# First head group of a decoder layer: turned rows in the output projection's bank, and another order of the first loads

## The reference, cut to what matters

```python
def _L0_attn_ref(x, wq, wk, wv, wo, q_scale, k_scale):     # x is the layer-normed input
    q = jnp.einsum('bse,ehd->bshd', x, wq)
    k = jnp.einsum('bse,ehd->bshd', x, wk)
    v = jnp.einsum('bse,ehd->bshd', x, wv)
    qn = rms_norm(q, q_scale)
    kn = rms_norm(k, k_scale)
    scores = jnp.einsum('bqhd,bkhd->bhqk', qn, kn)
    attn = jax.nn.softmax(scores, axis=-1)
    out = jnp.einsum('bhqk,bkhd->bqhd', attn, v)
    return jnp.einsum('bqhd,hde->bqe', out, wo)
x = x + _L0_attn_ref(_layernorm(x, axis=-1), ...)
```

## Time and profile before

| | |
|---|---|
| median of 3 runs | 2606.91 us (2603.4 to 2607.54) |
| profiled execution | 2602.67 us, its span 2600.9 us |
| TensorE busy | 2476.5 us, 95% |
| VectorE, ScalarE, GpSimd busy | 1544.2, 1343.1, 867.8 us |
| granted TensorE clock, mean | 0.98 of 2.4 GHz |

### The profile page before, as it was taken

How to read it: one execution, slowest core, us unless ns; L and a number is a source line. 1 busy time by engine, 2 the same in 40 slices (tenths; PEclk the granted TensorE clock), 3 DMA queues, 4 the chain that set the end, 5 groups by cost and what they waited for, 6 DMA issues and landing times.

```text
span 2600.9 us, 47418 instructions
## 1 busy us (share of the span) xinstructions
PE 2476.5 (95%) x16390; PEld 1334.4 (51%) x16390; DVE 1544.2 (59%) x3589; ACT 1343.1 (52%) x4098; POOL 867.8 (33%) x801
## 2 busy tenths in 40 slices
PE   6999999999999999999879999999999999999998
PEld 3555455555554555445454464464464464465466
DVE  7787756666666666667356545555554645645634
ACT  4555555555555555555446544454454554554433
POOL 2343333333333333333123324323323323422413
PEclk9999999999999999999869999999999999999999
DMA  5687777876787678787411001001001001000000
GB/s 155 151 183 169 154 154 158 175 166 148 156 173 156 154 157 185 167 193 162 125 35 34 32 3 35 16 2 37 17 2 37 12 6 37 4 14 24 7 17 8
DMA packets 455394, 235.29 MB, mean 90 GB/s; under 512 B 389096, under 2 KB 391784, under 8 KB 455144
## 3 DMA queue, kind: packets, MB, share of 16 engines
q1 hardware_dynamic: 455144, 232.08, 38.3%
HBM read 78.66 MB, written 32.77 MB: 43 GB/s over the span
## 4 chain that ended last, share of the span: by engine, by line
PE 84%; DVE 7%; ACT 4%; issue 3%; POOL 1%; DMA 1%; SPq 1%; DVEq 0%; POOLq 0%; ACTq 0%
PE ps L1474 22%; PE ps L1475 22%; PE ps L1476 22%; PE ps L1647 3%; PE ps L1648 2%; PE ps L1649 2%; ACT mem L948 2%; PE ps L1748 2%; PE ps L1657 1%; PE ps L1661 1%; PE ps L1659 1%; PE ps L1585 1%; PE ps L1736 1%; PE ps L1710 1%; PE ps L1730 1%
## 5 line engine op out<-in xcount | busy, mean ns | idle before, releaser
L1474 PE MATMUL ps<-mem 128*128 128x512 f16 (+6 forms) x3924 | 1203.5, 326 | 50.4 <-issue 23.3
L1475 PE MATMUL ps<-mem 128*128 128x512 f16 (+6 forms) x3924 | 1216.6, 325 | 0.0
L1476 PE MATMUL ps<-mem 128*128 128x512 f16 (+6 forms) x3924 | 1199.9, 325 | 0.0
L1474 PEld LDWEIGHTS ps<-mem 128*128 128x128 f16 (+3 forms) x3924 | 407.0, 104 | 370.8 <-issue 66.1
L1476 PEld LDWEIGHTS ps<-mem 128*128 128x128 f16 (+3 forms) x3924 | 408.4, 104 | 311.5 <-issue 9.2
L1475 PEld LDWEIGHTS ps<-mem 128*128 128x128 f16 (+3 forms) x3924 | 409.8, 104 | 300.4 <-issue 9.6
L736 POOL TENSOR_TENSOR mem<-mem 128x500 f32<-128x500 f32 (+1 forms) x231 | 268.6, 1163 | 358.3 <-ACT mem L1016 174.4
L686 POOL TENSOR_TENSOR mem<-mem 128x8 f32<-128x8 f32 x100 | 163.7, 1637 | 517.3 <-DVE mem L1090 517.3
L830 ACT ACTIVATE mem<-ps,mem 100x100 f32<-100x100 f32 x512 | 169.2, 345 | 223.2 <-DVE mem L1120 222.1
L1428 DVE TENSOR_TENSOR mem<-mem 128x500 f16<-128x500 f32 (+1 forms) x231 | 144.4, 648 | 179.7 <-ACT mem L998 175.3
L698 POOL TENSOR_TENSOR mem<-mem 100x400 f16<-100x400 f32 x128 | 158.8, 1241 | 173.1 <-ACT mem L840 173.1
(11 more groups left out here) (123 smaller groups left out, 3134.4 us busy)
## 6 DMA issues: line engine op xcount, KB each, us to landing
x<-mem SPq DMA_DIRECT2D x100, 256.0 KB, 2.9
mem<-x SPq DMA_DIRECT2D x75, 256.0 KB, 3.4
mem<-in_x SPq DMA_DIRECT2D x50, 256.0 KB, 3.6
mem<-x SPq DMA_DIRECT2D x12, 1000.0 KB
mem<-mem SPq DMA_DIRECT2D x32, 200.0 KB
out<-mem SPq DMA_DIRECT2D x6, 1000.0 KB
mem<-in_wq SPq DMA_DIRECT2D x16, 256.0 KB, 4.0
mem<-in_wk SPq DMA_DIRECT2D x16, 256.0 KB, 4.4
```

Of the source, the lines that this page charges most:

```text
L1474: pe.matmul(out_ap, ah, bh, start=(i == 0), stop=False)
L1475: pe.matmul(out_ap, ah, bl, start=False, stop=False)
L1476: mm = pe.matmul(out_ap, al, bh, start=False, stop=(i == len(pairs) - 1))
```

## The change

Rows are turned in the output projection's bank `ps_w` in place of the round of banks 0 to 3, so `UNITS` has only q and k. The turn waits for the adds of all output projections before it (`wo_before`), and an output projection waits for the `rows_lo` of all tiles turned before it (`rows_before`). `rows_lo` moves ahead of `scale_q` in VectorE's step. The eight quarters of q and k load in step -7, behind tile 1. Pieces q and k are split quarter by quarter, each with a semaphore of its own, on ScalarE and VectorE.

```diff
@@ -270,7 +270,7 @@
         ps = ctx.enter_context(nc.psum_tensor("ps", [P, 8, 512], F32))
         ps_v, ps_s, ps_w, ps_o = (ps[:, b, :] for b in range(4, 8))
 
-        names = ("ident0 ident half scales qks wld0 wld1 whi wlo xin0 xin1 xin2 bst mv var rstd xn lnT xhi "
+        names = ("ident0 ident half scales qks wq0 wq1 wq2 wq3 wk0 wk1 wk2 wk3 whq wld0 wld1 whi wlo xin0 xin1 xin2 bst mv var rstd xn lnT xhi "
                  "xlo qp kp sqq sqk ss ms rr qf khi klo qhi qlo qkT0 qkT1 vp ve vb0 vb1 s mx exp den rden "
                  "norm phi plo pz pT0 pT1 vlo o ohi olo w xr0 xr1 xr2 add st0 st1 st2")
         s = {n: sem("s_" + n) for n in names.split()}
@@ -301,12 +301,11 @@
 
         UNITS = []
         for n in range(FIRST_STEP, STEPS):
-            UNITS += [("rows", u) for u in turned_tile(n)]
             UNITS += [(m, u) for u in projected_at(n) for m in ("q", "k")]
 
         def bank(kind, u):
 
-            return ps[:, UNITS.index((kind, u)) % 4, :]
+            return ps_w if kind == "rows" else ps[:, UNITS.index((kind, u)) % 4, :]
 
         def bank_before(kind, u):
 
@@ -314,6 +313,15 @@
             return UNITS[i - 4] if i >= 4 else None
 
 
+        def wo_before(u):
+
+            return sum(len(summed_at(n)) for n in range(projected_step(u) - 1))
+
+        def rows_before(w):
+
+            at = [n for n in range(STEPS + 2) if w in summed_at(n)][0]
+            return sum(projected_step(u) - 1 <= at for u in range(TILES))
+
         def split_step(piece):
 
             hg, m = divmod(piece, 4)
@@ -321,7 +329,7 @@
 
         def load_step(piece):
 
-            return ((FIRST_STEP, FIRST_STEP, -4, -2)[piece] if piece < 4
+            return ((FIRST_STEP + 1, FIRST_STEP + 1, -4, -2)[piece] if piece < 4
                     else max(split_step(piece - 2) + 1, split_step(piece) - 4))
 
         def pieces_split(n):
@@ -537,7 +545,7 @@
                 if k >= 2:
                     sp.wait_ge(s["wlo"], k - 1)
                 sp.dma_start(stages[:, k % 2, e, :], piece_src(k)[:, e, :]
-                             ).then_inc(s[f"wld{k % 2}"], 16)
+                             ).then_inc(s[f"wld{k % 2}" if k >= 2 else f"w{'qk'[k]}{e}"], 16)
 
             def load_x(u):
                 if u >= 3:
@@ -764,8 +772,15 @@
 
         @block.scalar
         def _(act):
+            def split_first_hi(k):
+
+                for e in range(KC):
+                    act.wait_ge(s[f"w{'qk'[k]}{e}"], 16)
+                    act.activation(piece(k, True)[:, e, :], stages[:, k, e, :], ACT.Copy,
+                                   scale=W_SCALE).then_inc(s["whq"], 1)
+
             def split_hi(k):
-                act.wait_ge(s[f"wld{k % 2}"], 16 * KC * (k // 2 + 1))
+                act.wait_ge(s[f"wld{k % 2}"], 16 * KC * (k // 2))
                 if k >= 8:
                     act.wait_ge(s["w"], TILES * (k // 4 - 1))
                 act.activation(piece(k, True), stages[:, k % 2, :, :], ACT.Copy,
@@ -907,7 +922,7 @@
                 if 0 <= n + 1 < STEPS:
                     probs_hi(n + 1)
                 for k in pieces_split(n):
-                    split_hi(k)
+                    split_first_hi(k) if k < 2 else split_hi(k)
                 for k in b_pieces_split(n):
                     split_b_hi(k)
                 for u in projected_at(n):
@@ -1035,8 +1050,18 @@
 
         @block.vector
         def _(dve):
+            def split_first_lo(k):
+
+                for e in range(KC):
+                    dve.wait_ge(s["whq"], KC * k + e + 1)
+                    op = dve.scalar_tensor_tensor(out=piece(k, False)[:, e, :],
+                                                  in0=stages[:, k, e, :], scalar=W_SCALE,
+                                                  in1=piece(k, True)[:, e, :], op0=ALU.mult,
+                                                  op1=ALU.subtract)
+                op.then_inc(s["wlo"], 1)
+
             def split_lo(k):
-                dve.wait_ge(s["whi"], k + 1)
+                dve.wait_ge(s["whi"], k - 1)
                 dve.scalar_tensor_tensor(out=piece(k, False), in0=stages[:, k % 2, :, :],
                                          scalar=W_SCALE, in1=piece(k, True),
                                          op0=ALU.mult, op1=ALU.subtract).then_inc(s["wlo"], 1)
@@ -1225,16 +1250,16 @@
                     inverse_sum(n + 1)
                 for u in valued_at(n):
                     take_v_lo(u)
+                for u in turned_tile(n):
+                    rows_lo(u)
                 for u in projected_at(n - 1):
                     scale_q(u)
                 for u in projected_at(n - 1):
                     split_qk(u)
                 for u in normed_tile(n):
                     ln_rows(u)
-                for u in turned_tile(n):
-                    rows_lo(u)
                 for k in pieces_split(n):
-                    split_lo(k)
+                    split_first_lo(k) if k < 2 else split_lo(k)
                 for k in b_pieces_split(n):
                     split_b_lo(k)
                 for u in projected_at(n):
@@ -1480,11 +1505,14 @@
 
                 before = bank_before(kind, u)
                 if before:
-                    pe.wait_ge(s[{"rows": "xlo", "q": "qf", "k": "klo"}[before[0]]], before[1] + 1)
+                    pe.wait_ge(s[{"q": "qf", "k": "klo"}[before[0]]], before[1] + 1)
 
             def turn_rows(u):
                 pe.wait_ge(s["xn"], u + 1)
-                bank_free("rows", u)
+                if u:
+                    pe.wait_ge(s["xlo"], u)
+                if wo_before(u):
+                    pe.wait_ge(s["add"], wo_before(u))
                 for e in range(KC):
                     mm = pe.transpose(bank("rows", u)[:, e * P:(e + 1) * P], xin[:, u % 3, e * P:(e + 1) * P],
                                       ident[:, :])
@@ -1553,6 +1581,7 @@
                 pe.wait_ge(s["olo"], hg * NB + (t * P + P - 1) // S + 1)
                 if w:
                     pe.wait_ge(s["add"], w)
+                pe.wait_ge(s["xlo"], rows_before(w))
                 at = w * P % ORING
                 three(ps_w[:, :], [(oT_hi[:, h, at:at + P], oT_lo[:, h, at:at + P], out_hi[:, h, :],
                                     out_lo[:, h, :]) for h in range(HG)]).then_inc(s["w"], 1)
```

## The result

| | median | lowest to highest | runs |
|---|---|---|---|
| before | 2604.82 us | 2601.02 to 2611.19 | 17 |
| after | 2596.35 us | 2591.79 to 2601.28 | 17 |

The ratio is 0.9964, 95% interval 0.9957 to 0.9971: faster by 0.36%, where the prediction had 15.8 of 2606.9, 0.61%. By the medians 8.5 us went. The direction and the range held (2585 to 2599); the size is about half of the sum. All medians and ratios here are of executions at the usual granted clock, a mean of 0.975 to 0.982; one execution of experiment e7 and two of before, at 0.65 to 0.83, are left out. The profiled execution of after has a span of 2595.2 us, against 2600.9.

The account below looks back on a forecast made before the run. TensorE, busy 95% of the span, was taken as the bound, so only its stops count. 5.4 + 0.6 + 10.1 - 0.3 = 15.8 us off the 2606.91 median gave 2591.1 us, range 2585 to 2599.

Parts of the forecast that it names:

- Part 1: Opening: tile 1 loaded second and weights split by quarters start the first projection at 11.5 instead of 16.92: 5.4 us.
- Part 2: Behind the first projection: `rows_lo` moved ahead of `scale_q` saves 0.6 us; the wait ending at 55.32 ends 6.0 earlier.
- leave the clock at zero: Slow matmuls behind the longer stop (about 2 us) against the slow stretch behind 55.32 (1.7 us): counted as zero.
- Part 3: Five later waits for `scale_q` in the first group, 1.5 to 2.5 us each, go entirely: 10.1 us.
- neither a transpose nor an add takes their place: Rival, chance 0.10: transposes or adds are late instead of `scale_q`, leaving only the opening's 6.0 us: 2600.9.
- Part 4: Added waits between turning tiles and output projections in the shared bank: cost 0.3 us in all, upper end 5.1.
- list of what would make it wrong: Signs: turns waiting for adds, or output projections for `rows_lo`, over 1 us in total; new transpose stops; clock under 0.9.
- more than counted: Rival, chance 0.07: the 3.70 us stop for a late transfer and its slow matmuls go, 4 to 5 us more: 2586.5.
- theory A: From the experiments, not the forecast: the losses behind the first group are the scatter of executions.

Follow-up runs that it names:

- e7: Changed kernel, with rows turned in the next k projection's bank in steps without q and k projections, plus 34 one-element VectorE memsets ahead: 2587.30 us, ratio 0.9929.
- e4: Changed kernel, but in steps without q and k projections rows are turned in the next k projection's bank: 2592.57 us, ratio 0.9951.
- e12: Changed kernel with 34 memsets and rows turned in k's bank in steps without q and k projections, except tile 18: 2587.97 us, ratio 0.9927.
- e5: Kernel before with only the new banks and `rows_lo` order, plus six one-element VectorE memsets ahead of its loop: 2600.74 us, ratio 0.9979.
- e2: Kernel before with only the new banks and `rows_lo` order, loads and weight splits as before: 2595.97 us, ratio 0.9963.
- e3: Kernel before with only the new load order and split by quarters, old banks and `rows_lo` place: 2604.25 us, ratio 0.9993.
- e1: The changed kernel run again unaltered, for a second trace: 2592.57 us against 2606.28 before, ratio 0.9957.
- e6: Changed kernel, with rows turned in the next k projection's bank in steps without q and k projections, plus ten one-element VectorE memsets ahead: 2603.89 us, ratio 1.0.
- e8: Kernel before with only tile 1 loaded ahead of the weights, pieces split whole, banks as before: 2601.76 us, ratio 0.9986.
- e10: Kernel before with 40 one-element memsets ahead of VectorE's loop, nothing else: 2603.88 us, ratio 0.9992.
- e11: Kernel before with only the split by quarters, tile 1 still loaded behind the weights, banks as before: 2607.39 us, ratio 1.001.

## Why the prediction was right in direction and too high in size

**Part 1, the opening, was right** to 0.04 us, by its own steps: tile 1 right behind tile 0, quarters at 0.60 (measured 0.61), 7.7 for ScalarE's start, 8.9 for VectorE's, 11.5 for the projection. By the page "VectorE: DVE Perf Modes" of the Trainium skill, section "The TRN2 errata", the estimate was 11.75; three more instructions cost 0.15 us here and not the 0.47 of its fixed latency, since the quarters overlap when they follow each other, and the row decides: 11.54. The q piece was whole at 9.23 and not at 8.97, which cost nothing: ScalarE comes to the last quarter at 9.53.

**Part 2 was right in its chain.** The first value projection starts at 35.71 (35.7), after a stop of 3.20 (3 to 4). The scores came at 50.81, not 49.3: the seven matmuls from 36.66 to 39.22 took 0.63 us each, and the granted clock of 20 to 40 us is 0.91. In return the slow stretch that began near 56 us in the kernel before is gone, and tile 5 is turned at 54.26 in place of 60.15, 5.9 us earlier where the two parts had 6.0. So to leave the clock at zero was right in the sum, because the slow stretch behind 55.32 went, as the prediction had said it may. TensorE's timeline:

```profile
35.71 0.39 PE L1499 MATMUL ps<-mem 128*128 128x512 f16 x1 [3.20 <-DVE mem L1065]
...
50.81 0.22 PE L1499 MATMUL ps<-mem 128*100 128x100 f16 x1 [1.88 <-issue]
```

**Part 3 was right that the waits for `scale_q` go, all seven**, and that neither a transpose nor an add takes their place.

**Part 4 is the step that failed: the price of the output projection's wait for `rows_lo`, 0.1 us in the sum, measured 5.65.** It said that the `rows_lo` on which the output projection now waits "comes before `scale_q`, about 4 us ahead of it". In a step in which q and k are projected that is so: 24 matmuls lie between the turn and the output projection. Five steps that have an output projection (5, 9, 14, 18 and 23) have a turn but no projection of q and k. All engines, 94 to 97 us, after:

```profile
94.26 0.60 PE L1517 MATMUL ps<-mem 128*128 128x128 f32 x4
...
94.95 0.59 ACT L815 ACTIVATE mem<-ps 128x512 f16<-128x512 f32 x1
95.09 0.69 DVE L1169 SCALAR_TENSOR_TENSOR mem<-ps,mem 128x512 f16<-128x512 f32 x1
...
95.69 0.68 DVE L1100 TENSOR_TENSOR mem<-ps,mem 128x512 f16<-128x512 f32 x1
96.52 0.38 PE L1499 MATMUL ps<-mem 128*128 128x512 f16 x1 [1.13 <-DVE mem L1100]
```

Turn, high half, low half, output projection: only the mix of values stands beside a chain of two engines, and TensorE waits 1.13 us for the bank. Five of these are 5.65 us where 0.3 was taken for all of part 4. The prediction had compared the adds with the turns, one direction of the sharing, for 17 tiles; it compared the other direction for none. Its own list of what would make it wrong named these very waits, and e4, in which the five tiles turn elsewhere, has no such line. The direction that it did compare was right: no turn waited for an add.

**The rival "more than counted" came in part**, and not for its reason. The stop of 3.70 us became 1.76, because one of the five new waits stands ahead of it and the transfer runs meanwhile; the slow matmuls behind it went as well. e4 and e12 show the coupling: take the wait away and the stop and the slow clock are back, put it back and they go.

The first group then adds up: 5.4 + 0.6 + 10.1 - 5.65 = 10.45; the stop gives 1.9 (3.70 to 1.76), and the twelve small and five and a half large matmuls at 1.2 GHz behind it gave 12 x 0.04 + 5.5 x 0.21 = 1.6. That is 14.0; measured 13.8 and 14.4. That this is near the 15.8 of the sum is partly luck: 5.35 us of waits that it lacked stand against 3.5 of a stop that it had left at zero.

**A term was missing: VectorE's six instructions.** The prediction costed them at the place where they run. They also move VectorE's later loop by six instructions, and the stop in it comes three operations earlier and lasts 3.01 us a pass in place of 2.35. TensorE waits 10.8 us instead of 7.2 for this chain. The cost is 3.6 us by these waits, 3.9 by e5 against e2, and the part is 3.6 to 4.3 longer than before in the four kernels that have the quarters and no memsets. No row of group 1 could show it; the row that could, 2.35 us without a releaser in each pass, stands at 1964.36 in the trace of before, outside the stretches that the prediction read.

**The parts don't add.** Opening alone 3.2 us at the 25th add, banks alone 7.6 (9.0 in e5), together 13.8 and 14.4: the opening is worth 5 to 7 with the banks and 3.2 without. Without them the stops for `scale_q` and at the late transfer cost the clock, which depends on where they fall: 27 large matmuls at 1.2 GHz in e3, eight in the changed kernel. The prediction added its parts, which was right for the kernel that has both.

**Open.** Between 385 and 1508 us the shift changed by up to 4 us in either direction from kernel to kernel (after lost 3.9 there, e1 0.4, which is the same kernel). Stops that a transfer ends come and go in that part, and none was traced to the change: theory A holds for as much of it as e1 and after differ, and the rest is open. Open is also what makes a stop in the middle of a chain in the loop: no run tells the loading of code from another cause that goes by the number of instructions.

## What to carry to other kernels

When two users share a buffer, compare both directions of the wait in every kind of step, the steps that lack the work between them above all; a margin read from full steps says nothing of the empty ones. Where TensorE will stand for a transfer anyway, a wait ahead of that stop may be free, and two short stops can be cheaper than one of the same length because the clock holds. When a gain at one place is gone further on, count the matmuls at half clock in both traces before looking for a new wait. And if a kernel has a loop in its instruction streams, look in it for stops of an engine without a releaser before and after any change that alters the number of instructions ahead of it: here that was worth 16 us between one number and another, more than the change itself.

## What the runs showed of the hardware

- VectorE stood once in each pass of a loop but the first, 2.35, 3.01 or 4.20 us, at a place that moved by half an operation per instruction added ahead of the loop, and not at all with 34 or 40 added. The time of the kernel ranged over 16.6 us (e6 against e7), by that and by the copy below.
- A VectorE copy of 125x512 that started beside GpSimd's 125x2048 operation took 3.82 to 3.86 us in place of 0.43 and ended 0.3 us behind it, in each of the three passes of e6 that have the stop.
- Quarters back to back take 0.61 us each on VectorE and on ScalarE. The whole piece takes 2.29 on VectorE (e8), so four quarters cost 0.15 us more, and 0.53 more on ScalarE (1.91 whole).
- The same length of a stop of TensorE did or did not cost the clock, by where it fell. 2.49 us left it at 2.4 GHz at 172.21 (before) and was followed by eight large matmuls at 1.2 GHz at 168.65 (e8); 3.37 us left it at 2.4 GHz at 42.04 (e5) and was followed by eight at 1.2 GHz at 34.93 (e1). The shortest in the first group that was followed by matmuls at 1.2 GHz is 2.04 us (before, 55.32).
- Between runs of the same order of loads, the landing of q's last quarter scatters by 1 us: 8.27, 8.38, 8.93, 9.13 and 9.26 us with nothing but tile 0 ahead of the quarters (before, e10, e2, e5, e11), 8.49 to 9.61 with tile 1 ahead too. The prediction's 0.67 us for one more load can't be told from that.
